# Cross attention of a decoder layer: a score as three products of split queries and keys

## The reference

```
q = rope(rms_norm(x @ Wq.T))            # 16 heads of 128
k = rope(rms_norm(kv_in @ Wk.T))        # 4 heads of 128, kv_in = 375 context rows + 112 of x
v = kv_in @ Wv.T                        # 4 heads of 128
scores = (q . k) * SCALE                # each key head serves 4 query heads
attn = softmax(scores) @ v
out  = attn @ Wo.T
```

## Time and profile before

| | |
|---|---|
| median of the runs shown | 2627.21 us |
| the profiled execution | 2629.87 us, its span 2628.1 us |
| first and last score matmul | 1132.0 and 2057.2 us |
| busy share over the span | PE 85%, PEld 64%, DVE 50%, ACT 37%, POOL 33% |
| mean granted clock of TensorE | 0.931 |

### The profile page before, as it was taken

One profiled execution on the slowest core, in us unless ns is written; L12 is line 12 of the kernel. 1 busy time (PEld: TensorE's weight loads), 2 busy tenths in 40 slices (PEclk: granted clock), 3 DMA queues, 4 the chain that ended last, 5 costly groups with the idle time before them and its releaser, 6 DMA issues. The chain is left out here.

```text
span 2628.1 us, 35328 instructions
## 1 busy us (share of the span) xinstructions
PE 2226.5 (85%) x10448; PEld 1683.8 (64%) x10448; DVE 1324.5 (50%) x2900; ACT 969.1 (37%) x1976; POOL 858.9 (33%) x876
## 2 busy tenths in 40 slices
PE   5599999957888887589999999999999799838992
PEld 3588888845666665356666666666666477726771
DVE  3545555556555555344444444444444555534554
ACT  2323333333222221245445454544545422125661
POOL 2300000026555555433223232322322011135664
PEclk8899999978999998799999999999999899859996
DMA  7611221144333332312122122212221443135335
GB/s 273 181 51 36 64 63 35 36 138 138 113 115 115 115 113 84 124 45 62 55 56 76 55 62 66 62 55 57 59 55 36 153 111 96 56 124 176 105 107 188
DMA packets 293313, 243.76 MB, mean 93 GB/s; under 512 B 148226, under 2 KB 255218, under 8 KB 290802
## 3 DMA queue, kind: packets, MB, share of 16 engines
q1 hardware_dynamic: 276274, 205.64, 25.9%
q0 software_dynamic: 6496, 18.37, 2.5%
q10 hardware_dynamic: 10464, 18.77, 2.0%
HBM read 149.31 MB, written 93.42 MB: 92 GB/s over the span
## 5 line engine op out<-in xcount | busy, mean ns | idle before, releaser
L1865 POOL TENSOR_TENSOR ca_k<-ca_k 125x512 f32<-125x512 f32 x64 | 82.5, 1290 | 606.0 <-DVE ca_k L2098 606.0
L2113 DVE TENSOR_REDUCE ca_down<-ca_ps_s 112x1 f32<-112x487 f32 x256 | 164.5, 660 | 210.6 <-PE ca_ps_s L1937 208.9
L1937 PE MATMUL ca_ps_s<-ca_kT,ca_qT 128*112 128x487 f32 x512 | 233.3, 578 | 12.8 <-ACT ca_kT L2004 9.8
L75 PE MATMUL out_ps_y<-out_w_hi,out_o_hi 128*128 128x512 f32 x448 | 198.7, 444 | 37.2 <-DVE out_o_lo L1133 24.3
L2019 ACT ACTIVATE ca_prob<-ca_ps_s,ca_down 112x487 f32<-112x487 f32 x256 | 169.7, 666 | 151.2 <-DVE ca_down L2113 147.2
L75 PE MATMUL ca_ps_p<-ca_w_hi,ca_c_hi 128*125 128x512 f32 x384 | 188.2, 490 | 19.5 <-POOL ca_c_lo L1859 17.7
L1953 PE MATMUL ca_ps_o<-ca_pT,ca_v 125*128 125x448 f32 (+1 forms) x512 | 203.2, 539 | 0.6 <-ACT ca_pT L2026 0.6
L76 PE MATMUL out_ps_y<-out_w_lo,out_o_hi 128*128 128x512 f32 x448 | 189.2, 422 | 0.0
L77 PE MATMUL out_ps_y<-out_w_hi,out_o_lo 128*128 128x512 f32 x448 | 188.2, 420 | 0.0
L2095 DVE TENSOR_TENSOR ca_k<-ca_ps_p,ca_tab 125x512 f32<-125x512 f32 x64 | 44.2, 691 | 284.5 <-ACT ca_sq L1999 284.5
L1953 PEld LDWEIGHTS ca_ps_o<-ca_pT,ca_v 125*128 125x128 f32 (+1 forms) x512 | 97.2, 190 | 100.9 <-issue 100.1
(11 more groups left out here) (290 smaller groups left out, 5605.2 us busy)
## 6 DMA issues: line engine op xcount, KB each, us to landing
self_outT<-sa_ov SPq DMA_DIRECT2D x64, 224.0 KB, 2.4
out_o_raw<-self_outT SPq DMA_DIRECT2D x56, 256.0 KB, 3.2
cross_qT<-out_qt SPq DMA_DIRECT2D x56, 256.0 KB, 2.3
ca_qT<-cross_qT SPq DMA_DIRECT2D x64, 224.0 KB, 2.8
cross_outT<-ca_ov SPq DMA_DIRECT2D x64, 224.0 KB, 3.0
out_o_raw<-cross_outT SPq DMA_DIRECT2D x56, 256.0 KB, 3.2
ffn_raw<-in_expert_w SPq DMA_DIRECT2D x8, 1536.0 KB
ca_c_raw<-in_ctxT SPq DMA_DIRECT2D x16, 750.0 KB, 4.2
```

What stands on the lines that cost most here:

```text
L75: pe.matmul(out, a_hi, b_hi, start=start, stop=False)
L1865: pool.tensor_tensor(k1[0:m, :], k1[0:m, :], k2[0:m, :], ALU.add).then_inc(k_added.sem, 1)
L1937: pe.matmul(ps_s[j % 2][:, :], qT[i % 2][:, j, :], kT[par][:, i, :], start=True, stop=True).then_inc(scored.sem, 1)
L2113: dve.tensor_reduce(down[:, j:j + 1], ps_s[j % 2][:, :], AX.X, ALU.max, negate=True).then_inc(maxed.sem, 1)
```

## The change

Queries and keys are split, as x and the weights already are. A score becomes `mm3`: q_hi by k_hi, q_hi by k_lo, q_lo by k_hi, each an fp32r matmul of 488 columns (one padding column, filled once from the identity, since 487 is odd; maximum and exponential read 487). ACT makes the rounded queries (`high_q`, one step ahead, behind `square`) and its `keep_k` now writes `kT_hi`; DVE makes `kT_lo` (`low_k`, the last instruction of its step); POOL makes `q_lo` (`low_q`, behind the multiplication that finishes the key tile and ahead of `low`), in place over the loaded queries. `score` waits for `q_lo_ready` in place of the load, and for the DVE's `kT_ready` in place of ACT's.

```diff
@@ -1691,8 +1691,10 @@
         tab = [sb(f"tab{i}", [P, 4, 2, HD]) for i in range(2)]
-        qT = [sb(f"qT{i}", [P, HQ, S]) for i in range(2)]
-        kT = [sb(f"kT{i}", [P, KVH, KV]) for i in range(2)]
+        q_raw, q_lo = zip(*(ctx.both(f"q{i}", [P, HQ, S]) for i in range(2)))
+        q_hi = [sb(f"q_hi{i}", [P, HQ, S], F32R) for i in range(2)]
+        kT_hi = [sb(f"kT_hi{i}", [P, KVH, KV + 1], F32R) for i in range(2)]
+        kT_lo = [sb(f"kT_lo{i}", [P, KVH, KV + 1], F32R) for i in range(2)]
         v = [sb(f"v{i}", [P, 4, KVH * HD]) for i in range(2)]
@@ -1707,7 +1709,7 @@
         ps_p = [ctx.bank(f"ps_p{i}", P, D) for i in range(2)]
-        ps_s = [ctx.bank(f"ps_s{i}", S, KV) for i in range(2)]
+        ps_s = [ctx.bank(f"ps_s{i}", S, KV + 1) for i in range(2)]
         ps_t = [ctx.bank(f"ps_t{i}", P, 4, S) for i in range(2)]
@@ -1730,7 +1732,9 @@
         k_turned = ev("k_turned", 4, 1)
-        kT_ready = ev("kT_ready", 4, 1)
+        kT_hi_ready = ev("kT_hi", 4)
+        kT_ready = ev("kT_lo", 4, 1)
+        q_hi_ready, q_lo_ready = ev("q_hi", 4), ev("q_lo", 4)
         v_ready = ev("v_ready", 4, 1)
@@ -1773,6 +1777,11 @@
+        def after(b, i):
+            return (b, i + 1) if i < 3 else (b + 1, 0)
         @block.sync
@@ -1797,7 +1806,7 @@
                     wait(sp, scored, b, (i - 1) * HQ - 1)
-                sp.dma_start(qT[i % 2][:, :, :], qT_src[:, i * HQ:(i + 1) * HQ, bass.ds(b * S, S)])\
+                sp.dma_start(q_raw[i % 2][:, :, :], qT_src[:, i * HQ:(i + 1) * HQ, bass.ds(b * S, S)])\
                     .then_inc(q_in[i % 2].sem, 16)
@@ -1859,7 +1868,12 @@
-            def project(b, i, par):
+            def low_q(b, i):
+                wait(pool, q_hi_ready, b, i)
+                pool.tensor_tensor(q_lo[i % 2][:, :, :], q_raw[i % 2][:, :, :], q_hi[i % 2][:, :, :], ALU.subtract)\
+                    .then_inc(q_lo_ready.sem, 1)
+            def project(b, i, par, queries=None):
                 m = M[i]
@@ -1869,6 +1883,8 @@
                 pool.tensor_tensor(heads, heads, along(k_rstd[0:m, :], HD), ALU.mult).then_inc(k_normed.sem, 1)
+                if queries:
+                    low_q(*queries)
                 if i in (0, 1):
@@ -1876,10 +1892,12 @@
                 if more:
-                    project(b + 1, i, 1 - par)
+                    project(b + 1, i, 1 - par, after(b, i))
+                elif i < 3:
+                    low_q(b, i + 1)
             low(0, 0, 0)
-            batches(pool, project, step)
+            batches(pool, project, step, lambda: low_q(0, 0))
@@ -1930,11 +1948,12 @@
                 if j == 0:
-                    wait(pe, q_in[i % 2], b, i // 2)
+                    wait(pe, q_lo_ready, b, i)
                     if i == 0:
...
                 wait(pe, exped, b, i * HQ + j - 2)
-                pe.matmul(ps_s[j % 2][:, :], qT[i % 2][:, j, :], kT[par][:, i, :], start=True, stop=True).then_inc(scored.sem, 1)
+                mm3(pe, ps_s[j % 2][:, :], q_hi[i % 2][:, j, :], q_lo[i % 2][:, j, :], kT_hi[par][:, i, :],
+                    kT_lo[par][:, i, :], True, True).then_inc(scored.sem, 1)
@@ -2001,9 +2020,13 @@
                 wait(act, k_turned, b, i)
-                act.activation(kT[par][:, :, i * CT:i * CT + m],
+                act.activation(kT_hi[par][:, :, i * CT:i * CT + m],
                                ps_r[:, 0:KVH * m].rearrange("p (h t) -> p h t", h=KVH), ACT.Copy)\
-                    .then_inc(kT_ready.sem, 1)
+                    .then_inc(kT_hi_ready.sem, 1)
+            def high_q(b, i):
+                wait(act, q_in[i % 2], b, i // 2)
+                act.activation(q_hi[i % 2][:, :, :], q_raw[i % 2][:, :, :], ACT.Copy).then_inc(q_hi_ready.sem, 1)
@@ -2016,7 +2039,7 @@
                 wait(act, p_turned, b, n - HQ)
-                act.activation(prob[j][:, 0:KV], ps_s[j % 2][:, :], ACT.Exp, bias=down[:, j:j + 1],
+                act.activation(prob[j][:, 0:KV], ps_s[j % 2][:, 0:KV], ACT.Exp, bias=down[:, j:j + 1],
                                accum_out=total[:, j:j + 1]).then_inc(exped.sem, 1)
@@ -2054,6 +2077,8 @@
                     square(nb, i)
+                if more or i < 3:
+                    high_q(*after(b, i))
                 copy_pT(b, i, 0)
@@ -2067,7 +2092,9 @@
             k_sq.open(act)
-            kT_ready.open(act)
+            act.wait_ge(id_ready, 2)
+            for tile in kT_hi + kT_lo:
+                act.activation(tile[:, :, KV], ident[:, 0:KVH], ACT.Copy)
             v_ready.open(act)
@@ -2075,13 +2102,14 @@
             split(1)
-            batches(act, start, step)
+            batches(act, start, step, lambda: high_q(0, 0))
             copy_o(B - 1, 3)
...
             k_sum.open(dve)
+            kT_ready.open(dve)
@@ -2107,10 +2135,17 @@
+            def low_k(b, i, par):
+                m = M[i]
+                wait(dve, kT_hi_ready, b, i)
+                part = slice(i * CT, i * CT + m)
+                dve.tensor_tensor(kT_lo[par][:, :, part], ps_r[:, 0:KVH * m].rearrange("p (h t) -> p h t", h=KVH),
+                                  kT_hi[par][:, :, part], ALU.subtract).then_inc(kT_ready.sem, 1)
             def maximum(b, i, j):
...
                 wait(dve, scored, b, n)
-                dve.tensor_reduce(down[:, j:j + 1], ps_s[j % 2][:, :], AX.X, ALU.max, negate=True).then_inc(maxed.sem, 1)
+                dve.tensor_reduce(down[:, j:j + 1], ps_s[j % 2][:, 0:KV], AX.X, ALU.max, negate=True).then_inc(maxed.sem, 1)
@@ -2127,6 +2162,7 @@
                 squares(b, i)
+                low_k(b, i, par)
@@ -2141,6 +2177,8 @@
                 divide(b, i, 3)
+                if more:
+                    low_k(b + 1, i, 1 - par)
```

## The result

The changed kernel takes 2662.36 us (median of 4 runs, 2659.05 to 2664.87) against 2625.97 of before on the same chip (4 runs): 36.4 us more, a ratio of 1.0138 with a 95% interval of 1.0120 to 1.0155. It is slower, as forecast, inside the range given (2630 to 2672), but by 36 us and not by 22. Its profiled execution took 2661.94, 32.1 more than that of before.

The account below looks back on a forecast made before the run. Bound: the loop through POOL's multiplication, with scores 0 and 1 on its path. 45 inner steps +16.7, 15 batch starts +5.4, ends +1.3 - 1.5: +21.9 us, 2649 against the median of 2627.21; range 2630 to 2672.

Parts of the forecast that it names:

- What bounds: Key-tile loop, period 14.50 us: the path holds scores 0 and 1, not scores 2 and 3.
- the half: Second half of the loop, last `keys` matmul to end of POOL's multiplication: 6.77 us, set by DVE and POOL, unchanged.
- the second rival: Second half of the loop gets shorter as DVE's maxima start earlier: 9 to 15 us back, 2634 to 2640; chance 0.12.
- The product: Scores on PE: three fp32r matmuls take 0.67 us in place of 0.82, saving 0.31 a pair on the path.
- `low_q`: POOL's subtraction between multiplication and scores, taken as 1.04 us: scores start 0.68 us later in steps inside a batch.
- t0: Time mark in each step of the loop: the end of POOL's multiplication; scores' load was at 0.44 us after it.
- `low_k` at a batch's start: DVE's low keys hold up the scores in a batch's first step: +0.67 less 0.31, +0.36 a start, 5.4 us.
- Clock: Rival: PE's longer stops lower its clock to 0.91 over the stage, 48 us more, 2697; chance 0.06.
- Port: Rival: DVE's last divide shuts out POOL's subtraction, 21 us more (2670), or 64 more (2713); chance 0.07.
- Ends: Before the first score +1.3 us; in the last batch, shorter scores save 1.5 us.

Follow-up runs that it names:

- e2: Changed kernel with a fourth product, low query by low key, added in the scores of heads 0 and 1; 2693.84 us, ratio to before 1.0243.
- e3: Changed kernel with a fourth product, low query by low key, added in the scores of heads 2 and 3; 2662.82 us, ratio to before 1.0128.
- e1: Changed kernel with POOL's query subtraction moved to the start of its step and ACT's rounding behind head 1's exponential; 2627.89 us, ratio to before 1.0007.
- e4: Kernel before, fp32 scores, with the query rounding and subtraction added and waited for, the result unused; 2663.56 us, ratio to before 1.0132.
- e5: Changed kernel with POOL's subtraction cut in two, scores 0 and 1 waiting for the first half alone; 2645.35 us, ratio to before 1.0074.
- e6: Changed kernel with four useless matmuls on PE ahead of the waits at the starts of batches 1 to 15; 2647.14 us, ratio to before 1.0079.

## Why the prediction was right, and where it was short

- *What bounds.* The loop through POOL's multiplication, with scores 0 and 1 on it and scores 2 and 3 off it: shown by e2 against e3 and by the 6.77 us that did not move in the hardware loop (in the nine inner steps written out the half shrank from 6.70 to 6.66, the 0.05 at most that the second rival gave it). It is "off" by little: 0.43 more in scores 2 and 3 made the half 0.08 longer (e3).
- *The product.* 0.67 a score: the starts lie 0.22 apart and a pair gave 0.33 in the step above, 0.31 on average in e1. Right.
- *`low_q`.* The mechanism was right (e1, e4, e5), the term too small: I took 1.04 us from the subtraction over 500 elements, and it is 1.134. The multiplication's neighbour L1865 would have been the nearer row: 1290 ns for 512 elements (the page of before) is 2.52 ns for one, and 1134 for 448 is 2.53 (over a wider span the time is not in proportion: 224 elements take 661). Since the subtraction starts 0.04 ahead of t0, the load comes at t0 + 1.15 in the batches written out, 0.03 late; in the hardware loop it comes at t0 + 1.21 or 1.22. For these further 0.07, the larger part of the miss, I had no term, and no run shows what makes them. A step inside a batch grew by 0.45 and not by 0.37: 3.4 us of the shortfall.
- *`low_k` at a batch's start.* +0.36 was forecast, and the starts at full clock in the loop took 0.27 more (16.07 for 15.80). The load starts at t0 + 2.03, not 2.13. At full clock the 15 starts would have grown by 3.7 us together, where I had 5.4, and 1.3 more for the first score, which falls into the start of batch 0: that start grew by 0.18.
- *Clock.* This is the step that failed, and the largest part of the shortfall. I gave it 0.06 as a rival for the whole stage and nothing in the sum, because in the last batch of before stops of 1.43 us left the clock at 1.00. It fell at five of the 15 starts, each 1.4 to 1.6 us longer, 7.5 us, and at that of the last batch, 1.4. My argument took a stop's length alone; the stop that let the clock fall (1.37 us behind four transposes) is no longer than those that did not. e6 shows that the fall hangs on that stop (filled, it lets none of the 15 fall); why it comes at one start and not at the next, the runs leave open.
- *Port.* The subtraction did not stand still beside DVE: mean 1134 in the changed kernel, 1132 in e4. Nothing.
- *Ends.* The table's last two rows make +0.6 (-1.5 and +2.1), where I had -0.2 for the ends. The 1.5 us that I took off for the last batch did not come: to its last score it takes 38.40 us before and 38.38 in e6, where no clock falls; its first score starts 0.66 later there, which I had left out. What is left of the two rows is within what the other stages vary by.
- *The whole.* Between the spans of the profiled pair lie 31.8 us, 9.9 more than my 21.9. The clock's falls made 8.9, the inner steps 3.4, the saving in the last batch that did not come 1.5; against them the starts at full clock were 3.0 below the forecast, and the other stages 0.9. The range held the result, but it was not drawn for the clock, and that some terms erred the other way is luck. The rest, up to the 36.4 of the medians, no experiment speaks to.

## What to carry to other kernels

An engine that is 97% busy can still be waited past: ask at each point of the loop which wait ends last, and price an edit by the side of that point on which it stands. Cheaper matmuls were bought with a subtraction of 1.1 us on an idle engine, and its place cost more than twice what they gave (0.76 us a step against 0.31): put a helper's work where its engine idles, not between the hand-over and its reader. And where a change opens a stop in a matmul stream, look at the granted clock behind each such stop, one by one.

## What the runs showed of the hardware

- In the starts of batches 1 to 15 of the changed kernel the granted clock fell to the lower level at six, in or within 0.6 us behind stops of 1.34 to 1.37 us, and at nine with the same stops it did not; with four matmuls in the stop (0.3 to 0.5 us left, e6) it fell at none of the 15, and with the 0.7 to 0.9 us of before and e4 at none.
- At full clock an fp32r matmul of 488 columns costs 0.22 us from start to start, an fp32 score of 487 columns 0.82.
- POOL's subtraction takes 1134 ns for 448 elements a partition and 661 for 224; writing its result over one operand (the changed kernel, 1134) or elsewhere (e4, 1132) makes no difference.
